# Four of 104 gather groups of a graph network's linear passes, copied row by row by SP's and ScalarE's queues

## What is computed

```python
edge_index = jnp.stack([src, dst])
h = relu(layernorm(x));  x = x + L0(h, ...)   # attention, one head
h = relu(layernorm(x));  x = x + L1(h, ...)   # relation-typed sums
h = relu(layernorm(x));  x = x + L2(h, ...)   # two graph convolutions
h = relu(layernorm(x));  x = x + L3(h, ...)   # two attention layers, four heads

# L1: one row of a table for each edge, summed by target
msg = proj[src, rel_type]                     # proj: (3125, 8, 128)
agg = segment_sum(msg, dst, 3125)
out = relu(h @ root_weight + agg + bias)

# L2, twice: likewise, and a norm over the whole graph after each
msg = h[src] * norm[:, None]
out = segment_sum(msg, dst, n)
```

## Time and profile before

| | |
|---|---|
| median of 3 runs | 3715.31 us (3714.02 to 3720.5) |
| span of the profiled execution | 3712.7 us |
| beside the span, to the median | 2.6 us |
| PE, DVE, ACT, POOL busy | 64%, 46%, 31%, 66% |
| linear passes | about 740 to 1265, 1320 to 1845 and 1875 to 2400 us |

### The profile page before, as it was taken

How to read it: one execution, slowest core, us unless ns; L and a number is a source line. 1 busy time by engine, 2 the same in 40 slices (tenths; PEclk the granted TensorE clock), 3 DMA queues, 4 the chain that set the end, 5 groups by cost and what they waited for, 6 DMA issues and landing times.

```text
span 3712.7 us, 44858 instructions
## 1 busy us (share of the span) xinstructions
PE 2371.6 (64%) x12356; PEld 1813.4 (49%) x12560; DVE 1719.3 (46%) x4007; ACT 1147.3 (31%) x2849; POOL 2466.4 (66%) x2561
## 2 busy tenths in 40 slices
PE   3499888754444554444454444467787876777787
PEld 2477666333333433333343333346666664666665
DVE  4355555432232332222232222236777675666777
ACT  2366655400000110000000000025666642666662
POOL 1777775077777457777667777637777746777773
PEclk9987878955555565555555555557988887889987
DMA  4544332322122112212122212137666626666661
GB/s 94 87 85 85 85 78 48 142 53 53 53 53 53 39 51 53 53 53 53 45 59 53 53 53 53 43 115 197 181 181 182 180 65 187 182 179 178 181 178 31
DMA packets 345060, 356.77 MB, mean 96 GB/s; under 512 B 125614, under 2 KB 267637, under 8 KB 344821
## 3 DMA queue, kind: packets, MB, share of 16 engines
q0 software_dynamic: 93184, 219.12, 22.4%
q1 hardware_dynamic: 245494, 132.86, 13.5%
q10 hardware_dynamic: 6148, 1.93, 0.3%
HBM read 323.81 MB, written 30.05 MB: 95 GB/s over the span
## 4 chain that ended last, share of the span: by engine, by line
POOL 52%; issue 18%; PE 17%; DVE 5%; DMA 4%; ACT 2%; SPq 1%; DVEq 0%; ACTq 0%; POOLq 0%
POOL gathered_rows L485 32%; POOL gathered_rows L471 20%; PE QX L1192 7%; PE NU L1192 4%; PE MTB L1192 4%; DMA gathered_rows<-key_value_rows,src_index 1%; PE MID L1192 1%; DVE messages L738 1%; SPq L396 1%; DVE query_key_products L738 1%; DMA query_window<-gat_target_scores 0%; DMA open_tiles<-end_ahead_penalty 0%; PE MID L1225 0%; ACT window_distance L634 0%; DVE x_rows L738 0%
## 5 line engine op out<-in xcount | busy, mean ns | idle before, releaser
L1192 PE MATMUL NU<-gathered_rows 128*128 128x128 f32 x2496 | 635.7, 436 | 809.2 <-DMA gathered_rows<-gcn_rows,src_index 538.8
L1192 PEld LDWEIGHTS NU<-gathered_rows 128*128 128x128 f32 x2496 | 553.4, 326 | 991.6 <-issue 974.0
L471 POOL DMA_INDIRECT gathered_rows<-key_value_rows,src_index x832 | 822.8, 989 | 311.5 <-issue 247.5
L485 POOL DMA_INDIRECT gathered_rows<-gcn_rows,src_index x832 | 786.6, 945 | 344.9 <-issue 252.9
L738 DVE TENSOR_TENSOR sums_transposed<-sums_transposed,NU 128x512 f32 x624 | 426.7, 684 | 1241.7 <-PE NU L1192 1240.7
L471 POOL DMA_INDIRECT gathered_rows<-gat_rows,src_index x416 | 403.9, 971 | 208.8 <-issue 123.7
L485 POOL DMA_INDIRECT gathered_rows<-relation_rows,src_relation_index x416 | 393.3, 945 | 148.1 <-issue 126.5
L665 ACT ACTIVATE edge_node_onehot<-iota_window,dst_in_window_by_edge 128x128 f32<-128x128 f32 x1248 | 394.7, 386 | 30.4 <-PE MTB L1192 27.9
L1192 PEld LDWEIGHTS NU<-edge_node_onehot,messages 128*128 128x128 f32 x2496 | 388.1, 222 | 17.6
L1192 PE MATMUL NU<-edge_node_onehot,messages 128*128 128x128 f32 x2496 | 387.2, 306 | 13.0 <-issue 5.3
L1192 PE MATMUL MTB<-edge_node_onehot,edge_factors 128*8 128x128 f32 (+1 forms) x2496 | 359.8, 292 | 0.0
(11 more groups left out here) (257 smaller groups left out, 2624.4 us busy)
## 6 DMA issues: line engine op xcount, KB each, us to landing
query_window<-query_rows SPq DMA_DIRECT2D x832, 66.0 KB
dst_in_window_row<-dst_in_window SPq DMA_DIRECT2D x156, 256.0 KB
gathered_rows<-gcn_rows,src_index POOLq DMA_INDIRECT x832, 2.5
gathered_rows<-key_value_rows,src_index POOLq DMA_INDIRECT x832
relation_rows<-gathered_rows SPq DMA_DIRECT2D x25, 512.0 KB, 2.6
gathered_rows<-gat_rows,src_index POOLq DMA_INDIRECT x416
query_window<-gat_target_scores SPq DMA_DIRECT2D x416, 2.0 KB
gathered_rows<-relation_rows,src_relation_index POOLq DMA_INDIRECT x416, 2.5
```

What stands on the lines that cost most here:

```text
L471: pool.indirect_dma_start(out=rows_of(a, s)[:, t, :], out_offset=None, in_=a["table"], in_offset=bass.IndirectOffsetOnAxis(ap=srcI[:, TPG ...
L485: pool.indirect_dma_start(out=lrows[:, TPG * (K % LRING) + t, :], out_offset=None, in_=p["table"], in_offset=bass.IndirectOffsetOnAxis(ap= ...
L1192: return pe.matmul(o, l, r, start=start, stop=stop)
```

## The change

Groups 52 and 102 of each pass are fetched by SP, 53 and 103 by ScalarE, row by row. A row is a copy of its own: 512 bytes from a byte offset of the table, held in a register, to one partition. They go to buffers of their own, laid over the attention stages' `query_window`, and GpSimd leaves these groups out; its ring takes the 100 others in turn. DVE computes the byte offsets (row number times 512), once for relation rows and once, after the first pass, for source rows. PE waits for each tile's 128 copies by a count of 16 x 128 per pass.

```diff
+    BY_SP, BY_ACT = (52, 102), (53, 103)
+        row_at = sb("row_byte_offsets", [P, 4, TPG], i32)
+        flat_win = qwin[:].rearrange("p s t w -> p (s t w)")
+        own_rows = [flat_win[:, q * SPAN:(q + 1) * SPAN].rearrange("p (t d) -> p t d", d=D) for q in range(4)]
...
+        rows_in_sp = [[sem(f"rows_in_sp_{i}_{t}") for t in range(TPG)] for i in range(2)]
+        rows_in_act = [[sem(f"rows_in_act_{i}_{t}") for t in range(TPG)] for i in range(2)]
...
+        FETCHED = [(p, k) for p in range(3) for k in range(NG) if not by_rows(k)]
+        FETCH_NO = {pk: q for q, pk in enumerate(FETCHED)}
+        def linear_rows(p, k):
+            if k in BY_SP:
+                return own_rows[BY_SP.index(k)]
+            if k in BY_ACT:
+                return own_rows[2 + BY_ACT.index(k)]
+            q = FETCH_NO[p, k] % LRING
+            return lrows[:, TPG * q:TPG * q + TPG, :]
...
 # SP; ScalarE has the same with BY_ACT, 2 + i, rows_in_act, and waits on tstored itself
+            def rows_one_by_one(n, p):
+                table = p["table"].rearrange("n d -> (n d)").bitcast(u8)
+                tables_stored(n)
+                sp.wait_ge(S["row_at_ready"], 1 + min(p["k"], 1))
+                for i, k in enumerate(BY_SP):
+                    if p["k"]:
+                        sp.wait_ge(S["rows_used"], NG * (p["k"] - 1) + k + 1)
+                    for e in range(P):
+                        at = load_values(sp, row_at[e:e + 1, i, :], f"sp_row_{p['k']}_{i}_{e}", TPG, 4 * D * ((NV if p["k"] else NV * NREL) - 1))
+                        for t in range(TPG):
+                            sp.dma_start(linear_rows(p["k"], k)[e:e + 1, t, :].bitcast(u8),
+                                         table[ds(at[t], 4 * D)].unsqueeze(0)).then_inc(rows_in_sp[i][t], 16)
 # SP: after the table's stores, before the next table's
             store_tables(1, ...)
+            rows_one_by_one(1, LIN[0])
             store_tables(2, [(gcn_d, D, 0)])
+            rows_one_by_one(2, LIN[1])
             store_tables(3, [(gcn_d, D, 0)])
+            rows_one_by_one(3, LIN[2])
 # ScalarE: after the degree roots and before norm_tables(2, 2); after it; and after the rows of graph_norm(0)
...
 # GpSimd
                 for k in range(NG):
-                    K = NG * p["k"] + k
-                    if k >= LRING:
-                        pool.wait_ge(S["rows_used"], K - LRING + 1)
+                    if by_rows(k):
+                        continue
+                    q = FETCH_NO[p["k"], k]
+                    if q >= LRING:
+                        before, kb = FETCHED[q - LRING]
+                        pool.wait_ge(S["rows_used"], NG * before + kb + 1)
 # DVE
+            def row_offsets(idx):
+                for i, k in enumerate(BY_SP + BY_ACT):
+                    last = dve.tensor_scalar(row_at[:, i, :], idx[:, TPG * k:TPG * k + TPG], 4.0 * D, None, ALU.mult)
+                last.then_inc(S["row_at_ready"], 1)
+            row_offsets(relI)
             linear(LIN[0])
+            row_offsets(srcI)
             dve.memset(done_mark[:], 0.0).then_inc(S["numT_ready"], 1)
 # PE
-                    pe.wait_ge(lgathered[K % LRING], 16 * TPG * (K // LRING + 1))
+                    if not by_rows(k):
+                        q = FETCH_NO[p["k"], k]
+                        pe.wait_ge(lgathered[q % LRING], 16 * TPG * (q // LRING + 1))
                     for t in range(TPG):
+                        if k in BY_SP:
+                            pe.wait_ge(rows_in_sp[BY_SP.index(k)][t], 16 * P * (p["k"] + 1))
+                        if k in BY_ACT:
+                            pe.wait_ge(rows_in_act[BY_ACT.index(k)][t], 16 * P * (p["k"] + 1))
```

More of the change, by code:

```diff
@@ L693, in _, with rows_one_by_one @@
                                ).then_inc(S["deg_sqrt"], 1)
+            def rows_one_by_one(n, p):
+                table = p["table"].rearrange("n d -> (n d)").bitcast(u8)
+                for slot in range(NSLOT):
+                    act.wait_ge(S[f"tstored{slot}"], TOTAL[n][slot])
+                act.wait_ge(S["row_at_ready"], 1 + min(p["k"], 1))
+                for i, k in enumerate(BY_ACT):
+                    if p["k"]:
+                        act.wait_ge(S["rows_used"], NG * (p["k"] - 1) + k + 1)
+                    for e in range(P):
+                        at = load_values(act, row_at[e:e + 1, 2 + i, :], f"act_row_{p['k']}_{i}_{e}", TPG, 4 * D * ((NV if p["k"] else NV * NREL) - 1))
+                        for t in range(TPG):
+                            act.dma_start(linear_rows(p["k"], k)[e:e + 1, t, :].bitcast(u8),
+                                          table[ds(at[t], 4 * D)].unsqueeze(0)).then_inc(rows_in_act[i][t], 16)
+            rows_one_by_one(1, LIN[0])
             norm_tables(2, 2)
+            rows_one_by_one(2, LIN[1])
             def graph_norm(j):
@@ L1372, in linear @@
                     pe.wait_ge(S["s_ready"], SBASE[3 + p["k"]] + k + 1)
-                    pe.wait_ge(lgathered[K % LRING], 16 * TPG * (K // LRING + 1))
+                    if not by_rows(k):
+                        q = FETCH_NO[p["k"], k]
+                        pe.wait_ge(lgathered[q % LRING], 16 * TPG * (q // LRING + 1))
                     for t in range(TPG):
-                        last = mm(NU[k % 2][:, ds(off[t], P)], lrows[:, TPG * (K % LRING) + t, :], Sl[:, k % GPC, t, :],
+                        if k in BY_SP:
+                            pe.wait_ge(rows_in_sp[BY_SP.index(k)][t], 16 * P * (p["k"] + 1))
+                        if k in BY_ACT:
+                            pe.wait_ge(rows_in_act[BY_ACT.index(k)][t], 16 * P * (p["k"] + 1))
+                        last = mm(NU[k % 2][:, ds(off[t], P)], linear_rows(p["k"], k)[:, t, :], Sl[:, k % GPC, t, :],
                                   False, t == TPG - 1)
```

10 lines of the change are left out of this document (7 added, 3 removed).

## The result

The changed kernel takes 3840.47 us (median of 4 runs, 3826.76 to 3850.34) against 3714.66 us (4 runs, 3712.52 to 3720.5): ratio 1.0341, 95% interval 1.0312 to 1.0369. Forecast were 3671 us and a gain. The profiled execution has a span of 3836.4 us, 123.7 us over the 3712.7 of before.

A forecast was written before the change was run, and what follows sets the result against it. POOL's gathers were taken to bound the linear passes: 20.0 us saved less 4.9 at the end, 45.3 over three passes; 3712.7 - 45.3 + 0.5 = 3667.9 us of span, about 3671 measured; range 3652 to 3870.

The forecast's parts named there:

- A gather fewer is 1.25 us less: Linear passes: POOL's gathers set the pace at 1.249 us each, so 16 fewer save 20.0 us per pass.
- The price of a one-row copy: SP's and ScalarE's queues: between 0.21 and 0.45 us to issue a one-row copy; 0.21 taken from line 534.
- The milder form of rival A: Row copies on both queues cost 0.33 us, 2.05 a cycle; passes end later, +27 us, 3742; chance 0.08.
- rival A: Row copies on both queues at SP's wide price, 2.21 us a cycle: +152 us, 3867; chance 0.12 in full.
- rival B: Row copies at ScalarE's wide price, 0.45 us each, 2.53 a cycle: +392 us, 4107; chance 0.15.
- The cycle of one load and four copies, 1.57 us: Each queue's repeated unit, 256 per pass: 0.33 + 4 x 0.31 us, 402 us per pass, 95 us of slack.
- The rest of the cycle: Queue cycle apart from the load: four copies with move and gaps, 4 x 0.31 us.
- The limit of 1.96 and 1.94 us: Longest cycle at which SP (1.96) and ScalarE in pass 0 (1.94) still deliver groups 102 and 103 in time.
- Two groups behind the last gather, 4.9 us: End of each pass: PE still does groups 102 and 103 after the last landing, 2.47 us each, 4.9 given back.
- one of the two bounds that I had named: Pass-end cost of the two last groups: nothing if PE's clock, 0.50, rose; otherwise the whole 4.9 us.
- The middle burst costs nothing: After groups 52 and 53: POOL is up to 45 us ahead, so PE's two-group burst costs no time.
- DVE's offsets: Four small operations before pass 0, hidden; four for source offsets on the path once, 0.2 to 1.5 us, 0.5 taken.
- Rival C: POOL's gathers slow beside the queues' traffic, 31 to 53 us: 3702 to 3724; part way 0.07, upper end within 0.06.

The follow-up runs named there:

- pairs: Changed kernel with the register loads of two edges issued in a row, then their eight copies, on both queues: 3667.26 us, ratio 0.988 to the kernel before.
- eight registers: Changed kernel with one load of eight registers for eight copies and groups 94, 97 (SP), 98, 101 (ScalarE): 3662.94 us, ratio 0.9844 to the kernel before.
- all nine kernels of the table: The kernel before, the changed kernel and seven follow-up variants of it, compared by the lengths of their three linear passes, 506.1 to 570.5 us.
- the kernels with 4.5 copies per us and more: Changed kernel with loads of four edges in a row and groups 50, 97, 51, 101 (3672.66 us), or with fixed addresses and no loads (3696.53 regular, 3690.53 scattered).

## Why the prediction was wrong

It said faster and the kernel is slower. By its own steps:

- **A gather fewer is 1.25 us less: right.** 400 gathers in 500.9, 500.3 and 500.4 us, 1.252 apart. POOL was the bound, and where the queues are in time the passes shrink by 15.6 to 16.9 us (pairs).
- **The price of a one-row copy: right.** Taken 0.21, measured 0.228 on SP and 0.235 on ScalarE. The Trainium skill (DMA: Bandwidth & Descriptors, section on why a DMA increments its semaphore by 16) spoke against it if a row is cut to be spread; it was not cut. SP's queue shows 1616 packets for 807 copies in 400 us: 808 of 512 bytes and as many of 4 bytes. The milder form of rival A (0.33 a copy) and rival B (0.45) fall with it.
- **The cycle of one load and four copies, 1.57 us: this is the step that failed.** It is 1.98 on SP and 2.20 on ScalarE, and its largest mis-sized term is the load. "Of that 0.30 is the load (0.33 with its gap)" took over the price of a load that stands behind copies of 128 pieces. Behind one-row copies it is 0.565 on SP and 0.596 on ScalarE, 0.26 and 0.29 more in a cycle. I gave the copy bounds from both sides and the load none, since its row seemed to be the same instruction. The Trainium skill (DMA: Bandwidth & Descriptors, section Latency and other measured facts) gives a tensor_load a floor of about 600 ns and says that the compiler unrolls four times to hide it. If that is this instruction, the trace comes near it behind one-row copies and has half of it elsewhere (0.301 for window_base), so it is no floor here: the measurement decides. With it alone the cycle would have come out at an estimated 1.87 us, still under the limit.
- **The load by itself was not enough.** With its measured price alone the cycles would be 1.83 and 1.87 us, in time; with every other term as measured and the load at 0.30 they would be 1.72 and 1.91, in time too. It takes the load and the next point together to pass 1.96 and 1.94. The pairs and the eight registers cut the cost of the loads and the number of ScalarE's dear first copies at once, so no run parts the two; the shares here are read from the rows.
- **The rest of the cycle: too low by 0.15 (SP) and 0.33 (ScalarE).** The steps between copies have a mean of 0.33 us instead of 0.31 (the one after SP's first copy 0.38), and the first copy after a load costs 0.273 on SP and 0.467 on ScalarE; for the latter no row of before existed. SP: 0.33 + 4 x 0.31 = 1.57 forecast, 1.98 measured: +0.26 for the load and +0.15 for copies, moves and gaps. ScalarE: 2.20, +0.29, +0.23 for the first copy and about +0.1 for the rest.
- **The limit of 1.96 and 1.94 us: right.** SP at 1.98 is 1.56 us late, ScalarE at 2.20 is 59.5 us late. The forecast's terms give (2.20 - 1.94) x 256 = 67 us for ScalarE, 2.5 more as it starts at 750.5, and 5.6 less because PE itself is free for group 103 only at 1252.8 instead of 1247.2: 64 us. The 4 us that are left are rounding of the cycle (0.01 us in it is 2.6) and a landing shorter than 2.6: PE waits tile by tile, and starts on the group's first tile 0.2 us after ScalarE's last copy starts.
- **The result has the figure of rival A for ScalarE** (2.21 a cycle), but by coincidence: not its cause (dear copies throughout), and not for SP; so passes are longer by 46, 40 and 40 us instead of 54, 49 and 49.
- **Two groups behind the last gather, 4.9 us: too high.** In the run with pairs the matmuls end 5.03 us after the start of the third-last group, where one group took 2.05: 3.0 us for two. In that burst PE runs without a wait, its groups take 2.05, 1.66 and 1.05 us, and the granted clock goes from 0.50 (the 1.2 GHz level) to 1.00 (2.4 GHz) at 1253.41; a rise of the clock was one of the two bounds that I had named.
- **A landing that the sum left out.** Where GpSimd gathers group 103, PE starts on it 3.55 to 3.87 us after the start of the pass's last gather; where its last group is 101, it starts 2.58 to 2.71 us after. This holds in all three passes of all nine kernels of the table. So taking 103 off GpSimd gives back 1 us a pass more, for which the prediction has no term. Group 103 holds the last 389 of the 53125 edges and is padded to 512; whether that is why was not tested. For the first pass with pairs the parts then add up: the gathers save 519.8 - 500.9 = 18.9 us instead of 20.0, the time from the last gather's end to the last matmul's grows from 4.6 to 6.7, 2.0 us instead of 4.9, and the pass is 16.9 us shorter instead of 15.1. The 2.0 is the 3.0 of the burst less this 1 us.
- **The middle burst costs nothing: right,** even where group 53 is 20 us late.
- **DVE's offsets: right.** Four operations in 0.39 us (0.5 taken), on the path once.
- **Rival C, gathers beside the queues' traffic: hardly in this kernel** (a mean of 947 ns against 944) **but seen in the kernels with 4.5 copies per us and more.** Pairs and eight registers, at 4.3 and 4.4, stay just below.

So the mechanism of the forecast holds and 3667 us was there to be had. The sum failed in the cycle: a load's price taken from another neighbourhood, and on ScalarE the first copy behind it, left 0.02 us (SP) and 0.26 us (ScalarE) too much in a cycle that runs 256 times.

**Open:** why a load is dear behind one-row copies, even landed ones, and not behind wide ones; why ScalarE's first copy after it doubles; and by what single gathers become slow above 4.4 copies per us: rate and length of an uninterrupted series (eight against sixteen) were changed together, and the step from 4.4 to 4.5 is small for what it did.

## What to carry to other kernels

Price an instruction in the neighbourhood in which it will stand: the same register load costs 0.30 or 0.60 us by what was issued before it, and in a cycle that runs 256 times this and one dear copy made ScalarE 60 us late. Issue such loads in series (several loads, then all their copies) or load more registers at once. Put work that a slow queue brings where other work still comes behind it, and not at the end of a pass; and leave a queue that is in time as slow as it is: quicker ones took back 4 to 5 us a pass through the gathers, and without any pause between copies the gathers' rows came some 14 us late.

## What was not expected of the hardware

- A load of four registers: 0.30 us behind copies of 128 pieces or a load, 0.47 behind landed one-row copies, 0.56 (SP) and 0.60 (ScalarE) directly behind them; of eight: 0.78 and 0.83.
- ScalarE's first one-row copy after a load: 0.467 us, later ones 0.235; SP's 0.273 and 0.228.
- One-row copies without loads between them: up to 1.2 us, median 0.35, and gathers 1.258 to 1.280 us apart instead of 1.249, with their packets' share 24.1% instead of 20.1% and a group's rows there 15 to 18 us after the start of its last gather instead of 2.5 to 3.6.
- The rows of group 103, gathered last, are there 1 us later than those of group 101 where that is the last one gathered: 3.55 to 3.87 us after the start of its last gather against 2.58 to 2.71.
